# Moving additions, a norm, a mask and two transposes in a fused decoder layer

## The chip, the core and the metric

The kernel is one program on one core of a Trainium2 chip. The metric is device time in microseconds, from start to end of the execution. Before the change the median of three runs was 944.97 us (943.44 to 947.11).

## What is computed

The reference is one decoder layer on two sequences of 512 rows, each 512 wide, in float32. Each of its three parts is added to its input and then normalized over the row (mean 0, variance 1, eps 1e-5):

```python
x = layernorm(x + attn(x))          # 16 heads of 128, quantized weights times block scales
x = layernorm(x + cross(x, ctx))    # 1024 context rows, keys = values = context, top 54 scores kept
x = layernorm(x + ffn(x))           # silu(gate) * up, inner width 2048

# attn: q, k, v with bias; softmax(q k^T / sqrt(128)) v; output projection wo, bias bo
# cross: s = coef * (x Wq) ctx^T; s -= max; thr = 54th largest of the row; s below thr -> -inf;
#        softmax(s) ctx, times Wo
```

## The kernel before

Every operand of a product is split into a high and a low part, and a product is three matmuls (high x high, high x low, low x high). ScalarE writes the high part as a copy that rounds, VectorE or GpSimd the low part as a subtraction, and TensorE waits for both. There is no planner: each engine has its own instruction list, written out by hand in the functions `tensor`, `scalar`, `vector`, `gpsimd` and `sync` (the last issues all later loads), in which the same loops run. An engine works through its list in order; semaphores tie the lists together. So an instruction that waits holds up all that stands behind it on its engine.

The eight row tiles of 128 rows are `acc[:, r]`, r = 0 to 3 for the first sequence and 4 to 7 for the second. A chain of semaphore values for each r (`row_writers`) fixes the order in which its writers add to it.

**Attention** runs over 128 tiles, `i = 4 j + qt`: j is one of 32 (head, sequence) pairs, listed in `HB`, and qt a tile of 128 query rows. The last eight j take heads 12 to 15 of the first sequence, then of the second. In tile i TensorE projects q and k of j + 1 (`proj_qk`, for qt 0 and 1), transposes the exponentials of tile i (`transposed`, L713), multiplies them with v once per j (`attend(j - 1)`, at qt 0), multiplies two heads with wo (`proj_o(q, tt)`, L739 and L742, for a pair q of j's and row tile tt, at the places that `o_tile` gives) and computes the scores of tile i + 2 (L656 to L660). VectorE takes the maximum (`maximum(i + 2)`, L1496), ScalarE the exponential (L1024). `proj_o` gives two results, h = 0 and 1, each to be scaled by one over the softmax sum and added to its row tile. Either VectorE does both in one operation (`o_add`, L1522), or ScalarE scales into a buffer (`o_scale`, L1058) and GpSimd adds (L2068); `scaled_by_act` decides which. PSUM banks 4 to 7 are dealt out in a ring by `ring_plan`, in the order in which TensorE's list takes them; `claim` makes TensorE wait until the last user of a bank has read it. The bias bo with the part that comes from bv (`borow`, a product at i = 114) is added to the rows by GpSimd (`add_bias`, "bo2").

**The first norm** is `ln_stats` on VectorE (L1529, L1532), `ln_std` on ScalarE (a square root, L1071), `ln_rstd` and `ln_apply` on VectorE (L1536, L1540). Going from Exp to Sqrt and back loads an activation table each time. For rows 0 to 3 it stands in tiles 117 to 121, for rows 4 to 7 behind the loop. The transposes of the normalized rows (`row_T`, L747) and the query projection (L758 to L762) follow.

**Cross-attention.** `x_scores(n, hf)` (L773 to L776) gives 1024 scores for each row of tile n, copied out by `xs_copy` (L1175). The 54th largest is found by the search: for tile n, steps 0 to 12 alternate MAX8 (eight largest, L1561) and MATCH_REPLACE8 (take them away, L1569) on VectorE; step 13 is the exponential on ScalarE (L1185), 14 the mask with the sum on VectorE (L1572), 15 a reciprocal. Two tiles are searched at once, one even and one odd, one step of each in turn. The class `Search` hands out the steps: `run(k)` the next k, `until(n)` all up to the end of tile n, those of the other parity between them; `ready.add(n)` lets a tile in. VectorE and ScalarE each have a `Search` of their own, and their order differs where tiles become ready at other places. `px_T` (L845) transposes the masked weights, `px_high` and `px_low` split them, and `x_values` (L861 to L863) and `x_out` (L876) make the output; the left half of the first sequence (tiles 0, 1) goes ahead of the right half (tiles 2, 3).

**Feed-forward** is a loop over n = 2 to 32 (passes): `gate_up(n)` (L895 to L899), `gate_act` (L1326, L1333) and `gate_mul` (L1813, L1817), `down(n - 1)` (L909 to L911). Passes below 16 are for the first sequence, the rest for the second. In the passes 2 to 15 the second sequence's cross-attention is woven in: VectorE runs five search steps a pass behind its `gate_mul`, `px_T(4)`, `(5)`, `(6)`, `(7)` stand in passes 6, 7, 11 and 12, and `x_values` in 12 and 13.

Of the kernel before, what the change touches and what calls it, by code (L numbers as in the profile page):

```python
# [95 lines left out]
class Search:  # L96
# [28 lines left out]

    def until(self, n):
        out = []
        while n not in self.done:
            out += next(self.order, [])
        return out  # L130
# [82 lines left out]
def ring_plan():  # L213
# [9 lines left out]
    for i in range(4 * NJ):  # L223
# [12 lines left out]
        if i == 114:  # L236
            take("borow")
# [19 lines left out]
def row_writers(r):  # L257
# [4 lines left out]
    if b == 0 and tt < 2:  # L262
        out += [(12, 0), (12, 1), (13, 0), (13, 1), "bo2"]
    elif b == 0:
# [6 lines left out]
def scaled_by_act(q, tt, h):  # L271

    return h == 1 and (q < 13 or q == 13 and tt < 2)


def decoder_layer(nc, xT, xn, wq, sq, wk, sk, wv, sv, wo, so, bqk, bv, bo,
                  xwq, xwo, ctxT, ctxn, scal, wg, wu, wd, rq, rk, out):
    with ExitStack() as top:
# [84 lines left out]

        def cn(n):
# [71 lines left out]
        last_bias, last_sum = sig("last_bias"), sig("last_sum")  # L436
# [166 lines left out]
        def tensor(e, w):  # L603
# [175 lines left out]
            for i in range(4 * NJ):  # L779
# [19 lines left out]
                if i == 114:  # L799
# [141 lines left out]
            for n in range(2, 2 * NM + 1):  # L941
                if n == 7:
                    for hf in range(2):
                        px_T(5, hf, 6 + hf)
                if n == 12:
                    for hf in range(2):
                        px_T(7, hf, 6 + hf)
# [21 lines left out]
                if n < 2 * NM - 2:  # L969
# [11 lines left out]
        def scalar(e, w):  # L981
# [67 lines left out]
            def o_scale(q, tt):  # L1049
# [8 lines left out]
                e.activation(OBUF[:, n % 2], P[BANK["o", q, tt, 1]][:, :], ACT.Copy,  # L1058
# [39 lines left out]
            def conv_cn(k=1):  # L1098
                for _ in range(k):
# [4 lines left out]
                    if n < 2:  # L1104
# [4 lines left out]
                        w.wait_ge(*rows[7].at("bo2"))  # L1109
# [35 lines left out]

            def x2_high(r, direct):
# [19 lines left out]
            def xs_copy(n, hf, k):  # L1166
                w.wait_ge(*xsp.at((n, hf)))
                w.wait_ge(*coef_d.at())
                if n < 2:
                    w.wait_ge(*mul_p.at(LASTPIECE))  # L1170
                    w.wait_ge(*o_added(53))
# [39 lines left out]
            for i in range(4 * NJ):  # L1211
# [24 lines left out]
                if i == 114:  # L1236
# [5 lines left out]
                if (j, qt) == (29, 3):  # L1242
# [33 lines left out]
            xs_copy(3, 0, 0)  # L1276
            search(topk.run(1))
            x2_high(4, False)
            x2_high(5, False)
            xs_copy(3, 1, 1)  # L1280
            search(topk.run(2))
# [4 lines left out]
            search(topk.run(4))  # L1286
# [67 lines left out]
            search(topk.until(2))  # L1354
# [3 lines left out]
            search(topk.until(3))  # L1358
# [91 lines left out]
        def vector(e, w):  # L1450
# [83 lines left out]
            def ln_rstd(key, r0, n):  # L1534
                w.wait_ge(*std.at((key, r0)))
                e.reciprocal(rstd[:, r0:r0 + n], sd[:, r0:r0 + n]).then_inc(*rstds.up((key, r0)))  # L1536

# [152 lines left out]
            for i in range(4 * NJ):  # L1690
# [30 lines left out]
                if (j, qt) == (29, 1):  # L1721
                    ln_stats(1, [0, 1], row_writers(0)[-6])
                if (j, qt) == (29, 3):
                    ln_stats(1, [2, 3], row_writers(2)[-6])
                    ln_rstd(1, 0, 4)
                if j == 30 and qt < 2:
                    for r in (2 * qt, 2 * qt + 1):
                        ln_apply(1, r, 0)
# [16 lines left out]
            ot_low(NJ - 1)  # L1745
            search(topk.run(3))
            for tt in range(4):
                o_add(NJ // 2 - 1, tt, 0)
                o_add(NJ // 2 - 1, tt, 1)
                if tt == 1:  # L1750
                    ln_stats(1, [4, 5], (15, 1))
                    ln_rstd(1, 4, 2)
                elif tt == 2:
                    ln_apply(1, 4, 4)
# [455 lines left out]
```

## Time and profile before

| | |
|---|---|
| median of three runs | 944.97 us |
| the profiled execution, its span | 945.73 us, 943.9 us |
| busy: TensorE, its weight loads | 912.9 us (97%), 750.1 us |
| busy: VectorE, ScalarE, GpSimd | 593.0, 575.5, 491.8 us |
| mean granted clock of TensorE | 0.994 |

The page has one execution in six parts: busy time by engine, the span in 40 slices, DMA queues, the chain that ended last, the costliest groups of instructions, and DMA issues. Beside it the trace can be asked for the waits between engines, for stretches and for the instructions in order of time. All times in it count from the span's start. Attention ends at about 529 us, the masks of the first sequence at 606, the feed-forward loop begins at 634.

### The profile page before, as it was taken

The numbers are of one execution on the slowest core, as the hardware profiler recorded it, in microseconds if no ns is written. First come the engines' busy times: TensorE is split into PE (matmuls) and PEld (weight loads), VectorE is DVE, ScalarE is ACT, GpSimd is POOL, SyncE is SP. The second block draws the span as 40 slices with busy tenths as digits, with TensorE's granted clock in tenths as the row PEclk, the third lists the DMA queues.
The fourth block names the chain that finished last, engine by engine and source line by source line (L and its number), as shares of the span: only waits on it lengthen the run. The fifth ranks groups of instructions, "written<-read, shape, count | busy, mean of one in ns | idle before, by whom it ended". The sixth has DMA issues, their size and how long they took to land.

```text
span 943.9 us, 13220 instructions
## 1 busy us (share of the span) xinstructions
PE 912.9 (97%) x4440; PEld 750.1 (79%) x4440; DVE 593.0 (63%) x1066; ACT 575.5 (61%) x1142; POOL 491.8 (52%) x407
## 2 busy tenths in 40 slices
PE   8999999999999999999989889899999899999997
PEld 7788788887888877887868678798878788888885
DVE  5666966669666686658694899975878125411114
ACT  4667876678766787778874366533755534443333
POOL 4357752556526466477743467534764741354440
PEclk9999999999999999999999999899999999999999
DMA  7531230212302223123112303323433331343321
GB/s 202 157 104 53 86 89 1 61 58 75 100 1 54 64 74 84 46 72 86 54 43 83 90 23 101 104 76 100 124 91 99 104 112 41 112 122 94 94 83 44
DMA packets 46102, 76.97 MB, mean 82 GB/s; under 512 B 5584, under 2 KB 11216, under 8 KB 45776
## 3 DMA queue, kind: packets, MB, share of 16 engines
q1 hardware_dynamic: 45600, 75.68, 27.2%
q8 instruction: 40, 0.66, 0.3%
q10 hardware_dynamic: 432, 0.39, 0.2%
q14 instruction: 30, 0.25, 0.1%
HBM read 73.69 MB, written 2.36 MB: 81 GB/s over the span
## 4 chain that ended last, share of the span: by engine, by line
PE 40%; DVE 8%; ACT 2%; issue 2%; POOL 1%; ACTq 0%; DVEq 0%; POOLq 0%
PE p L895 6%; PE p L896 6%; PE p L899 6%; PE p L909 3%; PE p L910 3%; PE p L911 3%; DVE m L1561 1%; PE p L861 1%; PE p L862 1%; PE p L863 1%; PE p L776 1%; PE p L774 1%; PE p L773 1%; DVE acc L1522 1%; DVE st L1529 1%
## 5 line engine op out<-in xcount | busy, mean ns | idle before, releaser
L1983 POOL TENSOR_TENSOR V<-RAW,V 128x512 fp32r<-128x512 f32 x64 | 82.4, 1309 | 142.1 <-ACT V L1078 142.1
L1496 DVE TENSOR_SCALAR_CACHE_REDUCE JK<-p,ssc 128x512 bf16<-128x512 f32 x112 | 83.7, 747 | 112.9 <-PE p L660 112.9
L1024 ACT ACTIVATE PR<-p,nms,ssc 128x512 f32<-128x512 f32 x112 | 87.5, 781 | 60.0 <-DVE JK L1496 58.7
L2068 POOL TENSOR_TENSOR acc<-SX,acc 128x512 f32<-128x512 f32 x54 | 69.8, 1293 | 75.0 <-ACT SX L1058 51.8
L678 PE MATMUL p<-R 128*128 128x512 f32 x248 | 97.3, 392 | 0.8 <-DVE V L1489 0.8
L1983 POOL TENSOR_TENSOR C<-RAW,C 128x512 fp32r<-128x512 f32 x58 | 76.1, 1325 | 41.2 <-ACT C L1078 41.2
L1813 DVE TENSOR_TENSOR SX<-p,SX 128x512 f32<-128x512 f32 x32 | 22.1, 691 | 116.0 <-PE p L899 109.9
L1509 DVE TENSOR_TENSOR PT<-p,PT 128x512 fp32r<-128x512 f32 x128 | 87.4, 683 | 5.4 <-ACT PT L1043 5.2
L713 PEld LDWEIGHTS p<-ident,PR 128*128 128x128 f32 x512 | 62.4, 140 | 21.2 <-DVE PT L1509 6.6
L713 PE MATMUL p<-ident,PR 128*128 128x128 f32 x512 | 77.4, 274 | 1.0
L1043 ACT ACTIVATE PT<-p 128x512 fp32r<-128x512 f32 x128 | 75.8, 592 | 0.7 <-PE p L713 0.7
L680 PE MATMUL p<-R 128*128 128x512 f32 x192 | 75.1, 391 | 0.0
L1333 ACT ACTIVATE C<-SX 128x512 fp32r<-128x512 f32 x32 | 20.2, 632 | 76.3 <-DVE SX L1813 76.3
L656 PE MATMUL p<-QK 128*128 128x512 f32 x128 | 58.1, 454 | 0.0
L1951 POOL TENSOR_TENSOR RAW<-RAW,SCL 128x512 f32<-128x512 f32 x37 | 50.1, 1354 | 14.0 <-DMA RAW<-in_wk 7.9
L739 PE MATMUL p<-WO,OT 128*128 128x512 f32 x128 | 53.8, 420 | 2.8 <-DVE acc L1522 2.4
L678 PEld LDWEIGHTS p<-R 128*128 128x128 f32 x248 | 46.6, 188 | 11.8 <-issue 1.5
L1522 DVE SCALAR_TENSOR_TENSOR acc<-p,ri,acc 128x512 f32<-128x512 f32 x74 | 54.2, 734 | 1.5 <-PE p L742 0.9
L1970 POOL CROSS_LANE_REDUCE flag<-mag 128x1 f32<-128x2 f32 (+1 forms) x30 | 9.6, 320 | 85.7 <-ACT JA L1037 85.7
L895 PE MATMUL p<-V 128*128 128x512 f32 (+1 forms) x144 | 53.1, 376 | 0.6 <-POOL V L1983 0.6
L723 PE MATMUL p<-PT,V 128*128 128x512 f32 x128 | 50.5, 394 | 2.6 <-ACT PT L1043 2.6
L896 PE MATMUL p<-V 128*128 128x512 f32 (+1 forms) x144 | 52.6, 372 | 0.0
(243 smaller groups left out, 2735.9 us busy)
## 6 DMA issues: line engine op xcount, KB each, us to landing
RAW<-in_wg SPq DMA_DIRECT2D x32, 256.0 KB, 2.9
RAW<-in_wu SPq DMA_DIRECT2D x32, 256.0 KB, 2.7
RAW<-in_ctxn SPq DMA_DIRECT2D x32, 256.0 KB, 2.8
RAW<-in_wd SPq DMA_DIRECT2D x32, 256.0 KB, 2.8
RAW<-in_wq SPq DMA_DIRECT2D x19, 256.0 KB, 2.7
RAW<-in_wk SPq DMA_DIRECT2D x18, 256.0 KB, 2.7
RAW<-in_wv SPq DMA_DIRECT2D x16, 256.0 KB, 2.8
RAW<-in_wo SPq DMA_DIRECT2D x16, 256.0 KB, 4.7
```

What stands on the lines that cost most here:

```text
L678: e.matmul(ps, wh[:, kt], xh[:, kt], start=kt == 0, stop=False)
L680: e.matmul(ps, wh[:, kt], xl[:, kt], start=False, stop=False)
L713: m = e.transpose(ps[:, cols(kt)], PR[:, i % 2, cols(kt)], ident[:, :])
L895: e.matmul(ps, wl[:, cols(kt)], X3[b][:, 0, kt, c], start=kt == 0, stop=False)
L896: e.matmul(ps, wh[:, cols(kt)], X3[b][:, 0, kt, c], start=False, stop=False)
L1024: e.activation(PR[:, i % 2, :], P[i % 2][:, :], ACT.Exp, bias=nms[:, i % 4:i % 4 + 1], scale=ssc[:, 0:1] if HB[j][0] > 1 else SC, accum_ou ...
L1043: e.activation(PT[:, 0, :, cols(qt)], quad(P[2 + i % 2][:, :]), ACT.Copy).then_inc(*pt_hi.up(i))
L1496: e.tensor_scalar(JK[:, :], P[i % 2][:, :], ssc[:, 1:2] if HB[i // 4][0] > 1 else -SC, None, ALU.mult, ALU.min, accum_out=nms[:, i % 4:i % ...
L1509: e.tensor_tensor(PT[:, 1, :, cols(qt)], quad(P[2 + i % 2][:, :]), PT[:, 0, :, cols(qt)], ALU.subtract).then_inc(*pt_lo.up(i))
L1522: e.scalar_tensor_tensor(out=acc[:, r], in0=P[BANK["o", q, tt, h]][:, :], scalar=ri[:, 4 * (j % 4) + tt:4 * (j % 4) + tt + 1], in1=acc[:, ...
L1983: e.tensor_tensor(lo, RAW[:, slot[key], :], hi, ALU.subtract).then_inc(*c_lo.up(key))
L2068: e.tensor_tensor(acc[:, r], OBUF[:, (4 * q + tt) % 2], acc[:, r], ALU.add).then_inc(*rows[r].up((q, 1)))
```

## The change

- `o_tile`: `proj_o(13, 2)` and `(13, 3)` move from tiles 118 and 119 to 116 and 117. `ring_plan` follows, so the order of the banks changes.
- `scaled_by_act`: the h = 1 results of pair 13 (tt 2, 3), of pair 14 (all) and of pair 15 (tt 2, 3) go to ScalarE and GpSimd. From n = 56 on the buffers are CB and BO. `borow` moves from tile 114 to 110, the bo2 additions from 115 to 122 to 111 to 118, in another order of rows.
- The first norm: for rows 0 to 3 its statistics, root and applications come a tile earlier. For rows 4 to 7 VectorE makes only the factor and the bias (`ln_bias`), and ScalarE applies them (`ln1_apply`).
- Behind the loop, VectorE's search steps stand differently around the additions, and ScalarE's list is in another order, with the last conversion of context (`conv_ct(1, 7)`) later on ScalarE and GpSimd.
- Tiles 2 and 3 end their searches with `alone`, which takes all steps left of one tile, where `until` took steps of both.
- In the feed-forward, `px_T(5)` and `px_T(7)` stand behind the `gate_up` of their pass; in pass 12, `down(11)` comes ahead of `x_values`.

```diff
+    def alone(self, n):
+        z = n % 2
+        if n in self.done:
+            return []
+        out = [(n, s) for s in range(self.live[z][1], 16)]
+        self.done.add(n)
+        self.live[z] = [n + 2, 0]
...
+        return out
@@ o_tile
+    if j == 29:
+        return (13, 2 + qt) if qt < 2 else None
@@ scaled_by_act
-    return h == 1 and (q < 13 or q == 13 and tt < 2)
+    return h == 1 and not (q == 15 and tt < 2)
@@ tensor, feed-forward
             for n in range(2, 2 * NM + 1):
-                if n == 7:
-                    for hf in range(2):
-                        px_T(5, hf, 6 + hf)
-                if n == 12:
-                    for hf in range(2):
-                        px_T(7, hf, 6 + hf)
...
                     gate_up(n, (4, 5) if n % 2 or 6 <= n < NM else (6, 7))
-                if n in (6, 11):
+                if n in (6, 7, 11, 12):
                     for hf in range(2):
-                        px_T(4 if n == 6 else 6, hf, 6 + hf)
+                        px_T({6: 4, 7: 5, 11: 6, 12: 7}[n], hf, 6 + hf)
+                if n == 12:
+                    for tt in range(4):
+                        down(n - 1, tt)
@@ scalar, tile loop
-                if (j, qt) == (29, 3):
+                if (j, qt) == (29, 2):
                     ln_std(1, 0, 4)
@@ scalar, behind the loop
+            def ln1_apply(r):
+                w.wait_ge(*norm_bias.at(r - r % 2))
+                e.activation(acc[:, r], acc[:, r], ACT.Identity, bias=nms[:, r - 4:r - 3],
+                             scale=rstd[:, r:r + 1]).then_inc(*rows[r].up("ln1"))
...
             search(topk.run(1))
             ot_high(NJ - 1)
+            for n in range(4, 7):
+                conv_ct(1, n)
             xs_copy(2, 1, 1)
             search(topk.run(1))
-            for n in range(4, 8):
-                conv_ct(1, n)
-            search(topk.run(3))
+            for tt in (2, 3):
+                o_scale(NJ // 2 - 1, tt)
             act_table(ACT.Sqrt)
+            search(topk.run(1))
             ln_std(1, 4, 2)
+            ln1_apply(4)
+            ln1_apply(5)
+            xs_copy(3, 0, 0)
+            x2_high(4, False)
             search(topk.run(1))
             ln_std(1, 6, 2)
...
+            ln1_apply(6)
+            ln1_apply(7)
             x2_high(5, False)
+            search(topk.run(2))
             xs_copy(3, 1, 1)
+            conv_ct(1, 7)
@@ scalar and vector, fourth mask
-            search(topk.until(2))
-            search(topk.until(3))
+            search(topk.alone(2))
+            search(topk.alone(3))
@@ scalar, feed-forward
                 if n in (7, 12):
-                    px_pair(5 if n == 7 else 7)
+                    search(topk.until(5 if n == 7 else 7))
...
                     gate_act(n, (4, 5) if n % 2 or 6 <= n < NM else (6, 7))
+                if n in (7, 12):
+                    px_pair(5 if n == 7 else 7)
+                if n < 2 * NM:
                     conv_gu(n + 2)
@@ vector, behind the loop
             ot_low(NJ - 1)
+            search(topk.run(1))
+            for tt in range(2):
+                for h in range(2):
+                    o_add(NJ // 2 - 1, tt, h)
+            o_add(NJ // 2 - 1, 2, 0)
+            ln_stats(1, [4, 5], (15, 1))
+            o_add(NJ // 2 - 1, 3, 0)
+            ln_bias(4)
+            search(topk.run(1))
+            ln_stats(1, [6, 7], (15, 1))
+            ln_bias(6)
             search(topk.run(3))
-            for tt in range(4):
-                o_add(NJ // 2 - 1, tt, 0)
-                o_add(NJ // 2 - 1, tt, 1)
...
@@ gpsimd, tile loop
-                if 115 <= i <= 122:
-                    add_bias(i - 115, "bo2")
+                if 111 <= i <= 118:
+                    add_bias((4, 0, 1, 2, 3, 5, 6, 7)[i - 111], "bo2")
```

## Rows read from the trace of the kernel before

**Rows 1.** TensorE's waits over the whole span: who waits, for whom, us in total, times, longest.

```profile
PE p L845 <- DVE SX L1572: 5.5, 2, 2.9
PE p L747 <- DVE acc L1540: 4.0, 4, 1.3
```

**Rows 2.** Windows of 20 us: length, busy us (instructions) per engine, granted clock, DMA share, GB/s.

```profile
520.00:540.00 20.00, 17.76 (x76) 13.32 (x74) 17.39 (x29) 9.09 (x16) 10.07 (x8) 1.00 0.36 107
...
600.00:620.00 20.00, 15.68 (x102) 14.46 (x100) 19.89 (x33) 11.37 (x19) 14.26 (x12) 0.83 0.40 107
...
720.00:740.00 20.00, 17.40 (x78) 13.86 (x77) 10.86 (x15) 16.83 (x24) 12.66 (x10) 0.91 0.27 79
```

**Rows 3.** Timelines at the attention's end: start us, us, operation, [idle before, releaser].

```profile
466.06 0.75 DVE L1496 TENSOR_SCALAR_CACHE_REDUCE JK<-p,ssc 128x512 bf16<-128x512 f32 x1 [3.65 <-PE p L660]
...
477.60 1.28 DVE L1529 BATCH_NORM_STATS2 st<-acc 128x6 f32<-128x512 f32 x2
...
479.28 1.28 ACT L1071 ACT_TABLE_LOAD   x1 [1.42 <-DVE mv L1532]
...
482.44 1.28 ACT L1024 ACT_TABLE_LOAD   x1
...
484.23 1.09 PE L747 MATMUL p<-ident,acc 128*128 128x128 f32 x8 [1.31 <-DVE acc L1540]
```

**Rows 4.** One group of the page's fifth part, and ScalarE's timeline at the end.

```profile
L2068 POOL TENSOR_TENSOR acc<-SX,acc 128x512 f32<-128x512 f32 x54 | 69.8, 1293 | 75.0 <-ACT SX L1058 51.8
...
935.41 0.82 ACT L1438 ACTIVATE acc<-acc,nms,rstd 128x512 f32<-128x512 f32 x1 [0.61 <-DVE nms L1910]
```

**Rows 5.** Timelines of VectorE and TensorE behind the attention loop.

```profile
533.22 3.14 DVE L1522 SCALAR_TENSOR_TENSOR acc<-p,ri,acc 128x512 f32<-128x512 f32 x4
...
534.02 0.50 PE L739 MATMUL p<-WO,OT 128*128 128x512 f32 x1 [1.93 <-DVE acc L1522]
...
538.47 0.17 DVE L1536 RECIPROCAL rstd<-sd 128x2 f32<-128x2 f32 x1 [0.70 <-ACT sd L1071]
...
540.07 0.99 DVE L1540 TENSOR_SCALAR acc<-acc,mv,rstd 128x512 f32<-128x512 f32 x2
```

**Rows 6.** Timelines of the first two masks and their transposes.

```profile
558.91 1.22 DVE L1561 MAX8 m<-SCL 128x8 f32<-128x1024 f32 x1
...
562.50 2.23 DVE L1572 SCALAR_TENSOR_TENSOR SX<-SX,m,SCL 128x1024 f32<-128x1024 f32 x1
...
567.17 1.28 DVE L1572 SCALAR_TENSOR_TENSOR SCL<-SCL,m,SX 128x1024 f32<-128x1024 f32 x1
...
572.24 0.60 PE L845 MATMUL p<-ident,SX 128*128 128x128 f32 x4
```

**Rows 7.** Timelines of the third and fourth mask and the right-hand products.

```profile
594.23 1.20 DVE L1561 MAX8 m<-SX 128x8 f32<-128x1024 f32 x1
...
604.50 1.27 DVE L1572 SCALAR_TENSOR_TENSOR SX<-SX,m 128x1024 f32<-128x1024 f32 x1
...
605.93 1.94 PE L845 MATMUL p<-ident,SX 128*128 128x128 f32 x8 [2.91 <-DVE SX L1572]
...
608.98 0.55 PE L861 MATMUL p<-R,C 128*128 128x256 f32 x1 [1.11 <-DVE R L1832]
```

**Rows 8.** Timelines of the feed-forward's passes 10 to 12.

```profile
719.64 0.69 DVE L1813 TENSOR_TENSOR SX<-p,SX 128x512 f32<-128x512 f32 x1 [0.24 <-PE p L899]
...
727.70 1.06 PE L845 MATMUL p<-ident,SX 128*128 128x128 f32 x8
727.80 0.69 DVE L1813 TENSOR_TENSOR SX<-p,SX 128x512 f32<-128x512 f32 x1 [0.25 <-PE p L899]
...
730.22 1.28 ACT L1185 ACT_TABLE_LOAD   x1
731.51 1.15 ACT L1185 ACTIVATE SX<-SX,nmx 128x1024 f32<-128x1024 f32 x1
...
734.13 1.26 PE L845 MATMUL p<-ident,SX 128*128 128x128 f32 x8 [2.60 <-DVE SX L1572]
```

More of the change, by code:

```diff
@@ L261, in row_writers @@
     out = ["bo1"] + [(q, h) for q in qs for h in range(2)]
-    if b == 0 and tt < 2:
-        out += [(12, 0), (12, 1), (13, 0), (13, 1), "bo2"]
-    elif b == 0:
+    if b == 0:
         out += [(12, 0), (12, 1), "bo2", (13, 0), (13, 1)]
@@ L968, in tensor @@
                     x3_T(7, 7)
-                if n < 2 * NM - 2:
+                if n < 2 * NM - 2 and n != 12:
                     for tt in range(4):
@@ L1057, in o_scale @@
                     w.wait_ge(*masked_in[a].at())
-                e.activation(OBUF[:, n % 2], P[BANK["o", q, tt, 1]][:, :], ACT.Copy,
+                if n >= 56:
+                    w.wait_ge(*borowp.at())
+                    w.wait_ge(*rows[7].at("bo2"))
+                e.activation(scaled_at(n), P[BANK["o", q, tt, 1]][:, :], ACT.Copy,
                              scale=ri[:, 4 * (j % 4) + tt:4 * (j % 4) + tt + 1]).then_inc(*oscl.up((q, tt)))
@@ L1108, in conv_cn @@
                         w.wait_ge(*borowp.at())
-                        w.wait_ge(*rows[7].at("bo2"))
+                        w.wait_ge(*rows[7].at((15, 1)))
                     elif n < 5:
@@ L1285, in scalar @@
             conv_gu(0)
-            search(topk.run(4))
+            search(topk.run(2))
             for m in range(4):
@@ L1536, in ln_rstd, with ln_bias @@
                 e.reciprocal(rstd[:, r0:r0 + n], sd[:, r0:r0 + n]).then_inc(*rstds.up((key, r0)))
+            def ln_bias(r):
+                ln_rstd(1, r, 2)
+                w.wait_ge(*rstds.at((1, r)))
+                w.wait_ge(*sexp.at(127))
+                e.scalar_tensor_tensor(out=nms[:, r - 4:r - 2], in0=mv[:, r:r + 2, 0], scalar=-1.0,
+                                       in1=rstd[:, r:r + 2], op0=ALU.mult, op1=ALU.mult).then_inc(*norm_bias.up(r))
             def ln_apply(key, r, r0):
@@ L1722, in vector @@
                     ln_stats(1, [0, 1], row_writers(0)[-6])
+                if (j, qt) == (29, 2):
+                    ln_stats(1, [2, 3], row_writers(2)[-6])
                 if (j, qt) == (29, 3):
-                    ln_stats(1, [2, 3], row_writers(2)[-6])
                     ln_rstd(1, 0, 4)
-                if j == 30 and qt < 2:
-                    for r in (2 * qt, 2 * qt + 1):
-                        ln_apply(1, r, 0)
+                    ln_apply(1, 0, 0)
+                    ln_apply(1, 1, 0)
+                if i == 120:
+                    ln_apply(1, 2, 0)
+                    ln_apply(1, 3, 0)
                 if j == 30 and qt in (1, 2):
@@ L1826, in vector @@
             cross_add(1, 5)
-            search(topk.until(2))
-            search(topk.until(3))
+            search(topk.alone(2))
+            search(topk.alone(3))
             for hf in range(2):
@@ L1979, in add_bias, with add_scaled @@
                 e.tensor_tensor(acc[:, r], acc[:, r], BO[:, :], ALU.add).then_inc(*rows[r].up(which))
+            def add_scaled(q, tt):
+                r = 4 * HB[2 * q][1] + tt
+                w.wait_ge(*oscl.at((q, tt)))
+                w.wait_ge(*rows[r].before((q, 1)))
+                e.tensor_tensor(acc[:, r], scaled_at(4 * q + tt), acc[:, r], ALU.add).then_inc(*rows[r].up((q, 1)))
             def conv(key, hi, lo):
@@ L2063, in gpsimd @@
                 if o_tile(i) and scaled_by_act(*o_tile(i), 1):
[L2064 to L2069 removed]
+                    add_scaled(*o_tile(i))
                 if i >= 2:
@@ L2087, in gpsimd @@
                         conv_ct(1, n)
-            for n in range(4, 8):
+            for n in range(4, 7):
                 conv_ct(1, n)
-            for r in range(4, 8):
-                x2_low(r)
+            for tt in (2, 3):
+                add_scaled(NJ // 2 - 1, tt)
+            x2_low(4)
+            x2_low(5)
+            conv_ct(1, 7)
+            x2_low(6)
+            x2_low(7)
             conv_gu(0)
```

36 lines of the change are left out of this document (10 added, 26 removed).

## The prediction

> **What bounds the kernel now.** I read the windows of 20 us first, then TensorE's waits, then the timelines of the four engines around the largest of them. By the page's totals TensorE is busy 912.9 of 943.9 us, so only its 31 us of idle time, and the time at a low clock, can be won or lost. Its two longest kinds of wait are the transposes of cross-attention weights, which wait for the mask from VectorE (L845, 5.5 us in two waits), and the transposes of normalized rows, which wait for the first norm (L747, 4.0 us in four) [rows 1]. They lie in the stretches 520 to 540, 600 to 620 and 720 to 740, and in the last two the granted clock is also below 1 [rows 2]: after idle times of 2.9 and 2.6 us TensorE works at 1.2 instead of 2.4 GHz. Means of 0.83 and 0.91 over 20 us are 6.8 and 3.6 us at that level; the second costs half of it, 1.8, and of the first about 1.5 falls on work. Between 523 and 608 us VectorE has hardly a gap. It runs the top-54 search there, 1.16 us for each MAX8 or MATCH_REPLACE8, and the attention's additions and the norm lie in the same queue. So in that stretch a microsecond off VectorE is a microsecond off TensorE's wait at 605.93; outside of it, what counts is the order.
>
> **Attention end (tiles i = 110 to 122): costs 2.6, and 0.8 for the clock.** The borow product (0.46 us) and the eight bo2 additions only move; GpSimd, at 1.29 us each, has a hole of 4 us near 455 and time to spare after it. What it adds on GpSimd for head pairs 13 to 15 is eight such additions [rows 4], beside idle stretches of 10 us and more, each behind a scaling of 0.6 us on ScalarE. VectorE loses eight of 0.76 us, none of them on the path before i = 122. The gain sought is at 484.23, where TensorE waits 1.31 us for the norm of rows 0 and 1 [rows 3]; with the smaller ones behind it (0.2, 0.2, 0.4) some 2.3 us could go. Against it stand three new waits:
> - proj_o(13, 2) and (13, 3) come at i = 116 and 117. Each tile takes PSUM banks from a ring of four. Tile 116 now takes four (qk(30,0), av 28, two for proj_o), so qk(30,1) at the head of 117 gets the bank of qk(30,0), which qk_low frees. qk_low stands behind maximum(118), and that behind scores(118). Before, the maximum began at 466.06, after 3.65 us of waiting for that score [rows 3]; with proj_o (four products, 0.92, at 8.16 us for 36 in [rows 8]) ahead it is 466.98. The maximum takes 0.67 and qk_low 0.65, so the bank is free at 468.3, while TensorE wants it at 466.87: 1.5 us.
> - Tiles 118 and 119 keep only a transpose and a score, 1.15 us of TensorE. The loop score, maximum (0.75), exponential (0.9), transpose is longer than that: 0.7 us.
> - ln_std moves from i = 119 to 118, ahead of pt_high(119) on ScalarE. It waits for the statistics of rows 2 and 3, which are two pairs of bn_stats (1.28 a pair) and two aggregates late on VectorE. By the steps above: statistics at 478.5, then the table 1.28 and the root 0.3, as at 479.28 [rows 3], pt_high(119) at 480.65. attend(29) needs it. TensorE is there at 477.45 (468.4, tile 117 3.9, tile 118 1.15, the wait and tile 119 2.15, eight products 1.85): 3.3 us. Queued behind are pt_high(119), exponential(121) with its table load of 1.28, and qk_high(31, 0).
> The head of the row transposes is then reached at 487.9 instead of 484.23; the first 1.31 us lie inside that, the smaller waits (1.0) go: 3.7 - 1.0 = 2.6 later. Bounds: -2.3 (every old wait gone, none new) to +5. An idle time of 3.3 us is longer than those two after which the clock fell; each of these cost 1.5 to 1.8, here I take half, 0.8.
>
> The Trainium skill (ScalarE: Activation LUTs, "What ACT_TABLE_LOAD costs") gives about 1.28 us for the load and 1.38 us of drain with it. The row shows the 1.28 and the next instruction at once behind it, with no drain of that size; by the page's sum each of the two switches here would cost 1.38 more, and the total would be some 2.8 higher.
>
> **After the loop: gains 4.6.** Before, two more search steps stand ahead of the additions, so the first comes at 533.22 and TensorE waits 1.93 at 534.02 and 0.9 in pieces for banks [rows 5]. Now VectorE adds from 530.9, five in a row to 534.7, and TensorE has finished proj_o(15) by 534.5. ScalarE then has: two scalings to 535.25, table 1.3 and 0.2, root at 537.0, two applications at 0.82 each (the price of the same operation at 935.41, [rows 4]) to 539.2, xs_copy, x2_high(4), root at 541.05, two applications to 543.25, x2_high(5) to 544.2. The query projection, which began at 546.95, begins at 544.3; qx_high of the last part no longer stands behind the exponential of tile 0 (1.4 us of waits at 562). So TensorE comes to its mask transposes at 567.3 instead of 572.24 [rows 6].
> VectorE sets the rest. It loses two additions (1.5), four applications at 0.46 (1.8) and the wait of 0.70 at 538.47 [rows 5]; it gets two small products and waits for the two roots, 1.85 together. The last MAX8 of tile 0, ended at 560.05, ends at 557.8: 2.25 earlier. Two masks later I take 2.4, so tile 1's mask is ready at 566.0 and does not hold TensorE at 567.3 [rows 6]. From there VectorE holds nothing but steps up to 595.37 [rows 7], now 593.0. TensorE has come to x_out(0) at 591.5 and waits for ox_low, 1.9 us: part of the old wait, moved.
> With the search ending alone, tile 4's first MAX8 and its nmx (1.3) no longer precede mask 3, but VectorE waits for the exponential there, so only 0.7 is won at the mask, ended at 605.70 [rows 7] and now at 601.8 (2.4, 0.8 of idle before cross_add, 0.7). Behind it the replace and MAX8 of tile 4 ahead of px_low(3) (2.3) fall away, but ScalarE's px_high(3) ends only at 603.55. The right-hand products began at 608.98 [rows 7] and now at 604.35: 4.6. Their clock I leave as it was, since idle times of 2.0 and 1.45 us follow each other again. Bounds: 2 (ScalarE's longer queue loses what VectorE wins) to 7 (and full clock, 1.5).
> VectorE and GpSimd: the mask at 562.50 took 2.23 us beside a GpSimd conversion, the one at 567.17 took 1.28 [rows 6]. The Trainium skill (SBUF — State Buffer, "SBUF: two separate sides") says that a VectorE operation with two SBUF inputs and a GpSimd one that reads SBUF lock each other out for a whole instruction. By the row 0.95 us hangs on such a meeting; by the rule it can recur wherever the two meet, up to four masks here. The trace agrees with it at 562.50. I take one meeting, as before.
>
> **Feed-forward: costs 5.2.** px_T(5) and px_T(7) go behind their gate-ups. Two waits of 0.33 (px_T(5), 0.65 in all) and the 2.60 at 734.13 [rows 8] go. But the search's order changes too. Before, until(3) also did tile 4's steps 0 to 2, so even tiles led; now tiles 4 and 5 start level. Counting the steps: two in ln2, four, one, two, then five a pass, until(4) in pass 6. At the end of pass 10 both tiles 6 and 7 have done step 12, where before tile 6 had done its mask (step 14). So mask 6 falls into pass 11, behind gate_mul(11), and px_T(6) stands right behind gate_up(11) on TensorE. On ScalarE the alternation is turned: exponential 7 comes before 6, both behind gate_act(11) and conv_gu(13). From gate_up's end at 727.7 (T): gate_mul and the high half to T+1.4, two conversions to T+2.5, table to T+3.8 (before: 731.51, [rows 8]), exponential 7 to T+4.9, exponential 6 to T+5.9, mask 6 to T+7.2, px_T(6) at T+7.3. VectorE does 8.5 us of steps in pass 6, over its 7, and is still 0.5 late at pass 11: 7.8 us of wait. Against 2.6 and 0.65 that is 4.6 more. The clock after it: 1.8 before, 2.4 now, 0.6. Bounds: -3 (mask 6 in time) to +8.
>
> **Sum.** 2.6 + 0.8 - 4.6 + 4.6 + 0.6 = 4.0. The profiled execution took 945.73 us around its span of 943.9 (1.8 outside of it) and lies 0.8 above the median of 944.97: 949.7 as profiled, 949.0 as a median.
>
> **Rivals.**
> - *The order in the attention's end works.* For it: TensorE's waits at 484 to 491 are all late norms or banks freed by VectorE. Against: the bank of qk(30,0). If the three new waits are absent, 3.4 + 2.3 less: 943.3. Chance 0.17.
> - *Mask 6 is in time.* It would be if the steps ran ahead as before; the count speaks against it. The 5.2, and the old waits and clock of 2.6, 0.65 and 1.8, go: 938.8. Chance 0.13.
> - *Slower: the waits cost twice, by the clock.* One mechanism: at px_T(6) TensorE stands for more than 7 us and resumes at 1.2 GHz for the transposes, a down and part of the next gate-up, and the same happens before attend(29). Against: after the 2.6 us wait the low level lasted 3.6. If it lasts 6.8 on work after each, both cost 3.4 instead of 0.8 and 2.4, and the attention's end adds 0.6 of its upper bound: 953.2. It decides once the low level lasts over 4 us on work. Chance 0.2.
> - Forecast: 0.5, own range 946 to 952.
>
> A change under 0.5% (4.7 us) cannot be told from none here. Faster than 940.2 takes the second rival and a quarter of the first, by the bounds of the middle term: 0.17. Slower than 949.7 takes the third and a third of the forecast's range: 0.37. Within: 0.46. The range, 940.5 to 953.5, leaves out the lower part of the second rival and the tail of the third.
>
> **What would show it.** Right: a wait of over 1 us of L678 or L680 at i = 117 for qk_low; one of L723 near 478 for PT of ScalarE; no wait of L739 near 534; L845's wait at 605.93 about 2 us; one single wait of L845 of 7 to 8 us for the mask in the feed-forward, and none of 2.6. Wrong: if L845's longest wait there stays below 3 us, the count of search steps fails, and with it the sign; if the row transposes of the attention's end start before 484, the first part fails.

## The result and the profile after

The changed kernel took 954.15 us (median of 4 runs, 953.20 to 954.97) where the kernel before took 945.49 beside it (4 runs, 943.44 to 947.11): ratio 1.0083, 95% interval 1.0058 to 1.0107. It is slower: by 8.7 us by the two medians, by 7.8 by the ratio (0.0083 of 944.97, the base of the forecast; 5.5 to 10.1 by its interval). The profiled span is 951.4 us, 7.5 longer. The forecast was 4.0 more, a median of 949.0 with a range to 953.5. The median of 954.15 lies just above that range; by the ratio the base of 944.97 becomes 952.8, near its upper end.

TensorE's waits in the kernel after (what it waited for, total us, times, longest), against [rows 1]:

```profile
PE p L862 <- DVE SX L1612: 10.8, 2, 8.6
PE p L740 <- ACT PT L1057: 5.3, 5, 3.1
...
PE p L764 <- ACT acc L1165: 2.0, 2, 1.6
PE p L878 <- POOL C L2028: 1.7, 1, 1.7
PE p L695 <- DVE QK L1514: 1.6, 1, 1.6
```

The wait for the mask (L862, was L845) has doubled to 10.8 us, and one piece of it is 8.6. The wait of the row transposes for the norm on VectorE (4.0 in four) is gone from the top. In its place stand 3.1 us for PT (L740), 1.6 for the bank of q and k (L695), and 2.0 for ScalarE's norm of rows 4 to 7 (L764), nearly as much as the kernel before waited there for VectorE:

```profile
540.75 1.09 PE L747 MATMUL p<-ident,acc 128*128 128x128 f32 x8 [0.83 <-DVE acc L1540]
...
545.89 1.08 PE L747 MATMUL p<-ident,acc 128*128 128x128 f32 x8 [1.29 <-DVE acc L1540]
```

The windows, against [rows 2] (busy us by engine, then granted clock, DMA share, GB/s):

```profile
480.00:500.00 20.00, 16.64 (x80) 13.32 (x81) 13.52 (x30) 15.22 (x29) 4.52 (x5) 0.91 0.08 26
520.00:540.00 20.00, 19.90 (x91) 15.78 (x89) 16.17 (x24) 10.52 (x18) 11.41 (x9) 1.00 0.29 82
600.00:620.00 20.00, 15.26 (x102) 13.48 (x102) 17.39 (x31) 11.48 (x19) 13.96 (x11) 1.00 0.33 92
720.00:740.00 20.00, 11.39 (x49) 9.43 (x48) 13.08 (x19) 9.74 (x15) 6.94 (x7) 0.78 0.30 92
740.00:760.00 20.00, 19.65 (x88) 15.92 (x87) 1.39 (x2) 8.91 (x15) 12.41 (x11) 0.97 0.20 56
```

520:540 has filled up, 720:740 has lost 6 us of work, and a low clock has come to 480:500. In 600:620 it is gone in this profile, but not by the change: the second profile of the same kernel, among the experiments, has 0.83 there again.

To say where the 7.5 us are I cut both spans at three products that both kernels have: the first of attend(26) (L723, now L740), before any edit; the first of the query projection (L758, now L775), behind the attention's end; the first right-hand product (L861, now L878), behind mask 3. In the kernel before the first two are these; the third is in [rows 7]:

```profile
433.80 0.39 PE L723 MATMUL p<-PT,V 128*128 128x512 f32 x1
...
492.26 0.47 PE L758 MATMUL p<-R,WV 128*128 128x512 f32 x1
```

| stretch | before | after | more | forecast |
|---|---|---|---|---|
| start to attend(26) | 433.80 | 434.67 | +0.87 | 0 |
| to the query projection | 58.46 | 63.53 | +5.07 | +3.4 |
| to the right-hand products | 116.72 | 112.56 | -4.16 | -4.6 |
| to the end | 334.92 | 340.64 | +5.72 | +5.2 |

The first row is not of the change: no edited tile stands ahead of that product, and over the profiles of this case it went from 433.4 to 437.4. The two kernels differ there by the waits of the first products for converted data (L646: 2.2 us in all; 1.6 before, at L629); the profile with 437.4 has besides a granted clock of 0.66 in 10:20, where these two have 1.00. The other three rows add up to 6.63.

**Attention's end**, the timeline after (start, duration, engine and line, in brackets the idle time before it and what ended it), against [rows 3]:

```profile
434.67 0.39 PE L740 MATMUL p<-PT,V 128*128 128x512 f32 x1
...
469.38 0.47 PE L695 MATMUL p<-R 128*128 128x512 f32 x1 [1.61 <-DVE QK L1514]
...
475.01 0.51 PE L677 MATMUL p<-QK 128*128 128x512 f32 x1 [0.61 <-DVE QK L1514]
...
478.16 1.28 DVE L1561 BATCH_NORM_STATS2 st<-acc 128x6 f32<-128x512 f32 x2
479.83 1.28 ACT L1088 ACT_TABLE_LOAD   x1 [0.77 <-DVE mv L1564]
481.33 0.58 ACT L1057 ACTIVATE PT<-p 128x512 fp32r<-128x512 f32 x1
481.96 0.79 PE L740 MATMUL p<-PT,V 128*128 128x512 f32 x1 [3.15 <-ACT PT L1057]
...
490.47 1.04 PE L764 MATMUL p<-ident,acc 128*128 128x128 f32 x8
...
498.20 0.47 PE L775 MATMUL p<-R,WV 128*128 128x512 f32 x1 [0.77 <-DVE R L1709]
```

Every one of the three waits is there. L695 at i = 117 waits 1.61 for qk_low (forecast 1.5). In the short tiles TensorE waits 0.61 (forecast 0.7), though for the low part of q and k (L1514) and not for the loop through the exponential that the forecast named. The statistics of rows 2 and 3 end at 479.6, the table load stands ahead of pt_high(119) at 481.33, and attend(29) waits 3.15 (forecast 3.3). The row transposes come at 490.47, 5.4 later counted from attend(26).

**After the loop**, against [rows 5 to 7]:

```profile
542.74 1.27 POOL L2024 TENSOR_TENSOR acc<-BO,acc 128x512 f32<-128x512 f32 x1 [0.77 <-DVE acc L1554]
...
543.36 0.68 DVE L1575 SCALAR_TENSOR_TENSOR nms<-mv,rstd 128x2 f32<-128x2 f32 x1
...
547.21 1.28 POOL L2079 TENSOR_TENSOR R<-SG,R 128x512 fp32r<-128x512 f32 x1 [3.19 <-ACT R L1173]
...
547.55 0.97 DVE L1575 SCALAR_TENSOR_TENSOR nms<-mv,rstd 128x2 f32<-128x2 f32 x1
...
563.56 1.21 DVE L1601 MAX8 m<-SCL 128x8 f32<-128x1024 f32 x1
...
567.14 1.79 DVE L1612 SCALAR_TENSOR_TENSOR SX<-SX,m,SCL 128x1024 f32<-128x1024 f32 x1
...
608.41 1.19 PE L862 MATMUL p<-ident,SX 128*128 128x128 f32 x8 [2.19 <-DVE SX L1612]
...
610.76 0.36 PE L878 MATMUL p<-R,C 128*128 128x256 f32 x1 [1.17 <-DVE R L1871]
...
620.33 0.39 PE L878 MATMUL p<-R,C 128*128 128x256 f32 x1 [1.70 <-POOL C L2028]
```

The wait of 1.93 at L739 is gone. Mask 0 again meets a conversion on GpSimd (1.79 us; mask 3 in [rows 7] took 1.27), as was taken. The two small products of ln_bias (L1575) meet GpSimd too, which was not counted. Each begins while GpSimd works on operands in SBUF and ends 0.03 us after that operation: 544.04 after 544.01, and 548.52 after 548.49. In all eleven profiles that have ln_bias the two ends lie within 0.01 to 0.03 us of each other. So their 0.68 and 0.97 us are, by these rows, the rest of GpSimd's operation and not the work on 128x2 elements; a product that met none is in no profile. L862 still waits 2.19 for mask 3. A wait of 1.70 stands at 620.33, for a conversion on GpSimd, where the kernel before waited 0.29 at 618.58; the second profile of the changed kernel has none there.

**Feed-forward**, against [rows 8]:

```profile
729.72 0.67 DVE L1852 TENSOR_TENSOR SX<-p,SX 128x512 f32<-128x512 f32 x1
...
733.41 1.15 ACT L1207 ACTIVATE SX<-SX,nmx 128x1024 f32<-128x1024 f32 x1
734.46 1.13 ACT L1207 ACTIVATE SCL<-SX,nmx 128x1024 f32<-128x1024 f32 x1
735.63 1.28 DVE L1612 SCALAR_TENSOR_TENSOR SX<-SX,m,SCL 128x1024 f32<-128x1024 f32 x1 [3.85 <-ACT SCL L1207]
737.07 1.94 PE L862 MATMUL p<-ident,SX 128*128 128x128 f32 x8 [8.61 <-DVE SX L1612]
```

gate_mul(11) (L1852) is the first row; before it VectorE was at search steps, 1.3 us after the end of gate_up(11) at 728.46. The exponential of tile 7 (SX) comes first, that of tile 6 (SCL) second, then mask 6, then the transposes, after 8.61 us.

### The profile page after: what moved, and what is told of

It is laid out like the page before. It is cut to its first block, busy times and chain, and to the rows that moved or that the text cites. A ratio compares the mean times of both kernels' runs of the same rounds, so it can differ in the third digit from the quotient of the medians.

```text
span 951.4 us, 13233 instructions
## 1 busy us (share of the span) xinstructions
PE 911.5 (96%) x4440; PEld 748.8 (79%) x4440; DVE 586.8 (62%) x1056; ACT 578.2 (61%) x1150; POOL 501.1 (53%) x415
## 4 chain that ended last, share of the span: by engine, by line
PE 35%; DVE 12%; ACT 3%; issue 2%; POOL 1%; ACTq 0%; DVEq 0%; POOLq 0%
PE p L912 5%; PE p L916 5%; PE p L913 5%; DVE m L1601 4%; PE p L926 2%; PE p L927 2%; PE p L928 2%; DVE SX L1609 2%; DVE SCL L1609 2%; PE p L878 1%; PE p L880 1%; PE p L879 1%; PE p L893 1%; PE p L890 1%; PE p L891 1%
## 5 line engine op out<-in xcount | busy, mean ns | idle before, releaser
L2024 POOL TENSOR_TENSOR acc<-SX,acc 128x512 f32<-128x512 f32 x56 | 72.3, 1292 | 75.1 <-ACT SX L1075 51.8
L695 PE MATMUL p<-R 128*128 128x512 f32 x248 | 97.2, 392 | 2.4 <-DVE QK L1514 1.6
L1852 DVE TENSOR_TENSOR SX<-p,SX 128x512 f32<-128x512 f32 x32 | 22.1, 689 | 113.6 <-PE p L916 106.4
L673 PE MATMUL p<-QK 128*128 128x512 f32 x128 | 58.2, 455 | 0.0
L695 PEld LDWEIGHTS p<-R 128*128 128x128 f32 x248 | 46.5, 188 | 13.6 <-issue 3.4
L740 PE MATMUL p<-PT,V 128*128 128x512 f32 x128 | 51.4, 402 | 5.3 <-ACT PT L1057 5.3
L677 PE MATMUL p<-QK 128*128 128x512 f32 x128 | 51.2, 400 | 1.5 <-DVE QK L1514 1.5
L1554 DVE SCALAR_TENSOR_TENSOR acc<-p,ri,acc 128x512 f32<-128x512 f32 x66 | 48.3, 734 | 6.9 <-PE p L759 6.7
L912 PE MATMUL p<-V 128*128 128x512 f32 (+1 forms) x144 | 51.9, 368 | 0.7 <-POOL V L2028 0.7
```

Source lines behind the costliest of these rows:

```text
L673: e.matmul(ps, QK[:, s, 0, 0, c], QK[:, s, 1, 0], start=True, stop=False)
L695: e.matmul(ps, wh[:, kt], xh[:, kt], start=kt == 0, stop=False)
L912: e.matmul(ps, wl[:, cols(kt)], X3[b][:, 0, kt, c], start=kt == 0, stop=False)
L2024: e.tensor_tensor(acc[:, r], scaled_at(4 * q + tt), acc[:, r], ALU.add).then_inc(*rows[r].up((q, 1)))
```

## The experiments

The stretches in the tables are the three behind attend(26), in the order above. The start is left out of them. Times are medians beside the kernel before on the same chip.

**Norm of rows 0 to 3 back.**

```diff
-                if (j, qt) == (29, 2):
+                if (j, qt) == (29, 3):
                     ln_std(1, 0, 4)
```

and on VectorE the statistics, root and applications in their old tiles.

> The changed kernel with the norm of rows 0 to 3 (statistics, root, applications) in the places it had before; proj_o(13, 2) and (13, 3) stay at i = 116 and 117. Theory (the root ahead of pt_high(119) on ScalarE holds attend(29), 3.15 us, and the low clock behind that wait costs about 1.9 on work): both go, L740's wait falls below 0.5 us, the granted clock in 480:500 is 1.00, and a wait of about 1 us for the norm comes back at the row transposes; span about 947.5, ratio to the kernel before 1.004. Rival (the wait is only moved: the norm then holds the row transposes for as long): L764 waits 3 us or more there and the span stays at 950 to 951.5.

Measured: ratio 1.0045 (1.0030 to 1.0061), span 946.9; stretches 60.27, 112.50, 340.13. TensorE:

```profile
478.92 0.50 PE L740 MATMUL p<-PT,V 128*128 128x512 f32 x1 [0.80 <-ACT PT L1057]
...
486.34 1.08 PE L764 MATMUL p<-ident,acc 128*128 128x128 f32 x8 [0.28 <-DVE acc L1580]
```

attend(29) now waits 0.80 (below 0.5 was expected), the clock in 480:500 is 1.00, and the first stretch is 3.26 shorter. At the row transposes no wait of 3 us came back, nor the one of about 1 us that was expected (0.28): the rival is out.

**The same, and proj_o(13, 2) and (13, 3) back at 118 and 119** (the two lines added to `o_tile` go).

> The same, and proj_o(13, 2) and (13, 3) back at i = 118 and 119. Theory (the bank of qk(30,0) and the short tiles cost 1.6 and 0.7): L695's wait of 1.6 us at i = 117 goes, the first q projection begins at 492.3 to 492.8 as before (498.2 in the changed kernel), span about 945.5, ratio 1.002. Rival (the attention's end loses mainly by GpSimd's additions and ScalarE's scalings, which this kernel keeps): the q projection begins after 494.5 and the span is over 947.5.

Measured: ratio 1.0026 (1.0014 to 1.0037), span 946.0; 58.62, 112.53, 340.59.

```profile
484.84 1.08 PE L762 MATMUL p<-ident,acc 128*128 128x128 f32 x8 [1.49 <-DVE acc L1578]
...
492.88 0.47 PE L773 MATMUL p<-R,WV 128*128 128x512 f32 x1 [0.83 <-DVE R L1707]
```

The first stretch is 1.65 shorter still, and within 0.16 of the kernel before. So GpSimd's additions, the scalings and the moved borow product, which this kernel keeps, together neither cost nor bring anything here. The norm's wait at the transposes is back with 1.49 us (1.31 in [rows 3]): that is what the moves were to remove.

**The search in alternation again.** In ScalarE's list `until(3)` goes back behind px_high(2) and conv_cn as well, as in the kernel before.

```diff
-            search(topk.alone(2))
-            search(topk.alone(3))
+            search(topk.until(2))
+            search(topk.until(3))
```

> The changed kernel with the search as before: mask 2 and mask 3 ended in alternation with tiles 4 and 5. Nothing else. Theory (the order of search steps alone makes mask 6 late): the wait of 8.6 us before px_T(6) goes, and with px_T(5) and px_T(7) behind their gate-ups none of the old waits of 2.6 and 0.65 comes back; clock in 720:760 is 1.00; the third mask loses 1 to 2 us around 607: span about 942, ratio 0.998. Rival (the wait of 8.6 comes from VectorE and ScalarE being late by work, not by order): over 4 us of wait stay there, span 947 or more. Second rival (the old wait of 2.6 comes back): span 945.

Measured: ratio 0.9981 (0.9970 to 0.9993), span 941.2; 63.53, 113.97, 330.00.

```profile
720.00:740.00 20.00, 20.00 (x97) 16.52 (x97) 12.78 (x18) 16.05 (x23) 10.31 (x8) 1.00 0.27 80
```

TensorE is busy all of 720:740. Nothing over 0.66 us is left in the feed-forward, so moving px_T(5) and px_T(7) did remove the old waits, and the 8.6 came with the edit to the search. That it is the order of steps, and not ScalarE's list, is shown by the two kernels with a lead below, which keep that list. Ending mask 3 alone was worth 1.41 (113.97 against 112.56).

**Both.** The tiles and the norm of the attention's end as before (GpSimd's additions and the scalings stay), the search in alternation.

> Both: the attention's tiles and norm as before, the search in alternation; what stays of the change is the order after the loop (scalings and applications on ScalarE), GpSimd's additions, and px_T(5) and px_T(7) behind their gate-ups. Theory (the three parts add up: -5.9 and -9.5 against the changed kernel's span of 951.4): span about 936, ratio 0.992. Rival (part of the gain is given back at the next wait, as mask 3 or conv_cn): span 940 to 944, ratio 0.996 to 1.0.

Measured: 939.02, ratio 0.9925 (0.9908 to 0.9943), span 937.3; 58.58, 113.96, 330.04. The parts add up. Against the kernel before this is 0.12 more in the first stretch, 2.76 less in the second and 4.88 less in the third: what is left of the change is worth having.

**px_T(6) behind down(10).**

```diff
                 if n < 2 * NM - 2 and n != 12:
                     for tt in range(4):
                         down(n - 1, tt)
+                if n == 11:
+                    for hf in range(2):
+                        px_T(6, hf, 6 + hf)
```

> The changed kernel with px_T(6) behind down(10), no longer directly behind gate_up(11). Theory (TensorE stands only because mask 6 comes some 9 us after gate_up(11), and whatever is put ahead of it covers that much): the four products of down(10), 2.7 us, cover as much; the wait of 8.6 falls to 6.0, span 948.7, ratio to the kernel before 1.0055. Rival (px_T(7) is then as late, because px_high(6) and mask 7 follow later): a second wait before px_T(7), span 951 or more.

Measured: ratio 1.0060 (1.0046 to 1.0073); 63.58, 112.54, 338.45. (Its span, 952.0, has a start of 437.43.)

```profile
740.16 1.94 PE L862 MATMUL p<-ident,SX 128*128 128x128 f32 x8 [5.91 <-DVE SX L1615]
```

The wait falls from 8.61 to 5.91 as expected, and the last stretch by 2.2; no second wait came.

**The waits filled with products whose result is overwritten**, 13 ahead of attend(29), 38 ahead of px_T(6). The diff shows the second part.

```diff
+                if n == 6 and hf == 0:
+                    for x in range(38):
+                        e.matmul(ps[:, :], X3[0][:, 0, x % 4, cols(0)], X3[0][:, 0, x % 4, :], start=True, stop=True)
                 w.wait_ge(*pmask.at(n))
```

> The changed kernel with matrix products whose result is overwritten, put into the two long waits: 13 of 512 columns ahead of attend(29) and 38 ahead of px_T(6), about 3.0 and 8.2 us at full clock. Nothing that is computed changes. Theory (behind each long wait the low clock doubles the work for 3.4 to 4 us): the granted clock is 1.00 in 480:500 and 720:760, each place is 1.7 to 2.1 us shorter, span about 947.7, ratio 1.0045. Rival (the time is set by the waits alone, the low level costs nothing that another wait would not take): span 951, ratio 1.008.

Measured: ratio 1.0049 (1.0037 to 1.0061), span 947.7; 62.01, 112.54, 338.71.

```profile
480.00:500.00 20.00, 18.44 (x95) 14.55 (x94) 13.93 (x30) 16.57 (x32) 6.05 (x6) 1.00 0.12 37
720.00:740.00 20.00, 20.00 (x93) 16.41 (x92) 11.39 (x18) 10.80 (x17) 8.91 (x8) 1.00 0.24 76
740.00:760.00 20.00, 19.62 (x91) 16.04 (x90) 1.38 (x2) 9.77 (x16) 14.19 (x12) 1.00 0.34 96
```

The clock is 1.00 in all three windows. The first stretch is 1.52 shorter than in the changed kernel, the last 1.93: that is the price of the low clock alone at attend(29) and at px_T(6) in that execution, with waits and order unchanged.

**The kernel before, with masks 2 and 3 alone.**

> The kernel before, with one edit of the change: masks 2 and 3 end their searches alone. Theory (this edit by itself makes mask 6 late, and wins 1.4 to 1.9 at mask 3): one wait of 8 to 9 us for the mask before px_T(6), the wait of 2.6 before px_T(7) gone, clock below 0.85 in 720:740; right-hand products at 607.3 instead of 608.98; span 947.5 to 948.5, ratio 1.004. Rival (the wait arises only together with the moved px_T(5) and px_T(7)): no wait over 3 us in the feed-forward, span 942.

Measured: 950.31, ratio 1.0051 (1.0038 to 1.0064), span 947.9; 58.50, 115.33, 340.21.

```profile
688.35 1.06 PE L858 MATMUL p<-ident,SX 128*128 128x128 f32 x8 [1.77 <-DVE SX L1585]
...
731.28 1.15 ACT L1198 ACTIVATE SCL<-SX,nmx 128x1024 f32<-128x1024 f32 x1
732.34 1.13 ACT L1198 ACTIVATE SX<-SX,nmx 128x1024 f32<-128x1024 f32 x1
...
733.90 1.94 PE L858 MATMUL p<-ident,SX 128*128 128x128 f32 x8 [6.36 <-DVE SX L1585]
```

One edit makes the kernel before 4.0 us slower in the trace: it wins 1.39 ahead of the right-hand products and loses 5.29 behind. The rival is out. The wait before px_T(6) is 6.4, not 8 to 9: here ScalarE takes the exponential of tile 6 (SCL) first, and 1.77 us were already waited at px_T(5), so that VectorE was in time for gate_mul(11). Together it is 8.1.

**Masks 2 and 3 alone, and then a lead of three steps for tile 4**, with the attention's tiles and norm as before (so also in the three kernels behind this one). ScalarE's list of steps gets the same lead.

```diff
+    def lead(self, n, k):
+        s = self.live[n % 2][1]
+        self.live[n % 2][1] += k
+        return [(n, s + x) for x in range(k)]
...
+            search(topk.lead(4, 3))
             ln2(0, 2)
```

> The attention's tiles and norm as before, masks 2 and 3 alone as in the changed kernel, and then three steps of tile 4 by themselves behind px_low(3), so that the even tiles lead again. Theory (the lead of three steps is all that the feed-forward needs, and ending mask 3 alone wins 1.85 at 607): no wait over 1 us in 720:760, right-hand products near 605.4, span 935.5, ratio 0.9905. Rival (the three steps on VectorE ahead of the statistics make x3_T or ox_low late, and the gain is given back): span 937 to 939, as with the search in alternation (937.3).

Measured: 942.44, ratio 0.9969 (0.9957 to 0.9980), span 940.9; 58.57, 112.53, 336.43. The lead is all that the feed-forward needs (no wait over 0.7 there), but the rival was right about the place:

```profile
610.18 1.28 ACT L1093 ACT_TABLE_LOAD   x1 [5.06 <-DVE mv L1570]
...
617.78 0.58 PE L883 MATMUL p<-R,C 128*128 128x256 f32 x1 [3.00 <-POOL C L2032]
```

ScalarE waits 5.06 us for the statistics of rows 0 and 1, behind which its conversions stand, and TensorE then waits 3.00 for the last of them.

**The lead behind gate_mul(1).**

> As the kernel with the lead of three steps, but these three steps of tile 4 stand behind gate_mul(1), at 640, where VectorE is busy for only half of the time, and no longer ahead of the statistics of rows 0 and 1. Theory (the wait of 3.0 us for conv_cn at 617.8 came from those three steps: statistics, root and the conversions behind it in ScalarE's queue): L878's wait near 615 falls below 0.6, no wait over 1 us in 720:760, span 935.5, ratio 0.9905. Rival (the wait for conv_cn comes with the third mask ending earlier, its transfers being late): 2 us or more of wait at 615 to 618 stay, span 938 to 940.

Measured: 937.95, ratio 0.9911 (0.9891 to 0.9932), span 936.2; 58.57, 112.72, 330.22. The wait for the conversion is gone.

```profile
605.98 0.55 PE L883 MATMUL p<-R,C 128*128 128x256 f32 x1 [0.65 <-DVE R L1874]
```

This is the lowest median of all, 8.7 us below the kernel before beside it. Against the kernel with the search in alternation (0.9925) the intervals overlap; by the stretches it gains 1.07.

**The same with filled waits at 602 to 606.**

> The same with matrix products whose result is overwritten ahead of px_T(2) (9 of 512 columns) and ahead of the right-hand products (8 of 256 columns). Theory (the low clock at 600:620 costs the half of 1.8 to 3.4 us also there): clock 1.00 in 600:620, span 0.9 to 1.7 below that of the same kernel without them, ratio lower by 0.001 to 0.002. Rival (the products delay the transposes themselves or the clock stays low): no difference, or 0.5 longer.

Measured: 939.15, ratio 0.9921 (0.9901 to 0.9941), span 935.7; 58.63, 113.57, 330.00. The clock is 1.00 in 600:620, and nothing is won:

```profile
602.90 0.66 PE L870 MATMUL p<-ident,SX 128*128 128x128 f32 x4 [0.74 <-ACT R L1348]
...
615.26 0.39 PE L886 MATMUL p<-R,C 128*128 128x256 f32 x1 [1.70 <-POOL C L2037]
```

At full clock TensorE runs into a wait of 1.70 for the same conversion, and the fillers push the right-hand products back by 0.85. By the stretches it is 0.69 longer; the rival was right.

**Norm of rows 4 to 7 on VectorE**, in the kernel with the lead behind gate_mul(1).

> The kernel two above, with the norm of rows 4 to 7 applied by VectorE, as before the change, behind the same statistics; the two small products go. Theory (moving the application to ScalarE wins nothing: the product took 0.68 and 0.97 on VectorE where a pair of applications took 0.99, and ScalarE's pair takes 1.52): the first q projection of these rows begins 0.5 to 1 earlier, mask 3 within 0.4 of where it was, span within 0.7 of that kernel. Rival (as the prediction counted, VectorE gets 1.85 back by it and VectorE sets mask 3): mask 3 is 1 to 1.8 later and the span with it.

Measured: 940.41, ratio 0.9935 (0.9913 to 0.9958), span 937.7 (start 435.87); 58.58, 113.01, 330.24.

```profile
540.70 1.08 PE L769 MATMUL p<-ident,acc 128*128 128x128 f32 x8 [1.01 <-DVE acc L1582]
```

The query projection of these rows begins 1.54 earlier (0.5 to 1 was expected) and the right-hand products come 0.29 later, counted from the first query projection. So the move of the norm to ScalarE is worth 0.3 us. The medians differ by 2.5, which the intervals do not separate; 1.2 of the spans' difference is the start.

**The changed kernel again.**

> The changed kernel once more, with nothing edited. Theory (of the 7.5 us between the two profiled spans 0.9 fell before the first edited tile, where both programs are the same, and only 6.6 belongs to the change): ratio to the kernel before 1.007, from the start to the attend(26) product 433.4 to 434.5 us as in the others, 63.5 from there to the first q projection, 112.5 to the right-hand products, 340.1 to 340.6 behind. Rival (the changed kernel really is slower by 8.7, some of it in the head of the program): ratio 1.0085 to 1.010, and a head of 434.7 or more.

Measured: ratio 1.0096 (1.0079 to 1.0113), span 952.2, start 433.54; 64.63, 112.53, 341.50. Both expectations failed: the ratio is the rival's, but the head is not late, and the three stretches add up to 8.56 more than the kernel before, where the first profile had 6.63. The windows from 482 to 488, and the one at 600:

```profile
482.00:484.00 2.00, 2.00 (x6) 1.52 (x5) 0.64 (x2) 1.99 (x5) 0.42 (x1) 0.50 0.00 0
484.00:486.00 2.00, 2.00 (x6) 1.54 (x5) 0.00 (x0) 0.08 (x1) 0.85 (x1) 0.50 0.07 9
486.00:488.00 2.00, 2.00 (x11) 1.64 (x10) 0.32 (x1) 1.20 (x2) 0.00 (x0) 0.86 0.34 122
...
600.00:620.00 20.00, 16.65 (x95) 15.12 (x96) 17.40 (x31) 11.43 (x19) 13.95 (x11) 0.83 0.33 92
```

Here attend(29) began at 480.85, behind the same wait of 3.1 us, and the low level lasted 5.7 us of work, till 486.6. In the first profile it lasted 3.3, from 481.96 to 485.3 (1.28 us at half clock in 484:486, by its mean of 0.68). The same program took 1.96 more: 1.10 in the first stretch, 0.45 from the right-hand products to px_T(6), with the low level at 610:616, and 0.41 behind it, where the low level lasted 5.1 us and not 4.2.

## Why the prediction was right and wrong

- **Sign and places were right.** All three terms have their sign, and each wait named under "What would show it" stands within 0.9 us of its size. Of the others ox_low's was off: 1.9 at x_out(0) was forecast, 0.72 measured.
- **The term that was sized wrong most plainly is the clock in the attention's end**, "here I take half, 0.8"; no reason is given for the half. Filling the wait gave 1.52; against the second execution of the same program it is 2.62 (64.63 against 62.01). The price had to be taken from [rows 2], in full: 1.8.
- **"The smaller waits (1.0) go" failed too.** The row transposes were 5.37 later, the query projection 5.07: 0.3 of it went. The norm's waits did go, but L775 now waits 0.77 for x2_low. That wait is 0.82 and 0.83 with the norm back in its place, so it does not come from the norm: x2_low waits there for x2_high, which stands on ScalarE behind an exponential, and TensorE reaches it sooner, having lost the bank wait of 0.42 that the kernel before had at 490.71. These two make 1.4 of the 1.67 by which the first term fell short. The gross shift, 3.7, was right: 5.37 less 1.52 of clock is 3.85. By parts the norm cost 1.74 and its clock 1.52, and proj_o's place 1.65 (forecast 2.2 for the bank and the short tiles).
- **After the loop** 4.16 for 4.6. The order brought 2.75 (4.16 less 1.41). VectorE's two small products and waits, taken at 1.85, measured 0.56 + 0.68 + 0.71 + 0.97 = 2.92. The products' part, 1.65, is the time for which they met GpSimd; the prediction named such meetings for the masks alone. Ending mask 3 alone was worth 1.4 in each of three pairs. The low clock of [rows 2] in 600:620, which I left as it was, is worth little: at full clock TensorE waits for GpSimd's conversion instead, and the second execution lost 0.45 by it.
- **Feed-forward** 5.72 for 5.2. The count of steps was right, shown by undoing the edit, by making it alone, and by giving the lead back. The wait was 8.6 instead of 7.8: VectorE was 1.3 late at gate_mul(11), where I took 0.5. The clock was 1.9 (2.4 taken). What the kernel before loses there against the search in alternation, 334.92 - 330.0 = 4.92, is the 2.60 and the 0.65, and 1.67 are left, near the 1.8 of its clock; no run separates that rest.
- **The third rival** (the waits cost twice, by the clock, 953.2) named the right thing and too high a price. Its point of decision, a low level of over 4 us on work, was passed at three of four places: at px_T(6) in both profiles (4.2 and 5.1 us) and at attend(29) in the second (5.7), but not in the first (3.3). The two prices together were 3.45 us in the first execution and 4.95 in the second (2.62, and 2.33 from px_T(6) to the end against the filled waits), between the 3.2 of the forecast and the 6.8 of the rival. The median, 8.7 more, fits executions like the second, with 8.56. The mean granted clocks say the same: 0.992 in the first profile, the fastest of its four runs, 0.987 to 0.990 in the other three and in all four of the second time. At which places these lose it was not seen. So of the distance between the 4.0 of the forecast and the measured median some 2.6 us are its terms, by the first profile; for the rest the longer low clock of the other executions is the likely cause.
- The other two rivals are out: the attention's end did not gain (o_back shows it at par at best), and mask 6 was not in time.

The Trainium skill (TensorE: Matmul & The Clock Gate, "HAM oscillation — how this bites in real kernels") says that a wait for data lets the engine fall back, so that the next work starts cold. The trace agrees at attend(29) and px_T(6), with 1.5 and 1.9 us. The Trainium skill (ScalarE: Activation LUTs, "What ACT_TABLE_LOAD costs") gives 1.38 us of drain beside the load; the load at 479.83 ends at 481.11 and the root starts at 481.13, so it does not show here either.

## What to carry over

Work that is moved ahead on one queue is ahead of everything that stands there: a root with a table load moved one tile forward held the transposed exponentials that TensorE needed, for more than the wait it was to remove. Where two engines walk through the same order of steps, a local shortcut in it changes every later place; count to the end of the program, or give the lead back where the engine has time. Price a wait of TensorE like these, of 3 us or of 8, as the wait plus 1.5 to 2.6 us of low clock, and filling it with idle products is worth that only if nothing else waits behind, as the conversion did at 615. When a small operation of VectorE takes several times what its size suggests, look at what GpSimd does in the same moment before taking its time for a price.

## What the runs showed of the hardware

- The low clock behind the same wait (3.15 and 3.12 us) in the same program lasted 3.3 us of work in one execution and 5.7 in the other, and cost 1.1 us more; a single profile does not give its price.
- 38 products of 512 columns without use held TensorE at 2.4 GHz through a wait of 8.6 us and brought 1.9 us back.
- On VectorE a scalar_tensor_tensor of 128x2 elements with both inputs in SBUF took 0.68 and 0.97 us beside a GpSimd operation with its inputs in SBUF, and ended 0.01 to 0.03 us after it, in each of eleven profiles; a reciprocal of 128x2 took 0.17 beside the same operations.
